# Attention nodes: normalising the context in the transposed layout instead of transposing it back and forth on TensorE

## What is computed

```python
for c in range(6):
    q = ew[c, 0] * (nodes[in_q] @ We[eq] + be[eq])
    k = ew[c, 1] * (nodes[in_k] @ We[ek] + be[ek])
    v = ew[c, 2] * (nodes[in_v] @ We[ev] + be[ev])
    scores = einsum('bqhd,bkhd->bhqk', q @ Wq[c], k @ Wk[c]) / 4
    ctx = einsum('bhqk,bkhd->bqhd', softmax(scores), v @ Wv[c])
    nodes[c] = act_w[c] * (ctx @ Wo[c]) + q
x = x + layernorm(nodes[5]) * ln_g + ln_b
```

## Time and profile before

| | |
|---|---|
| median of 3 runs | 1112.06 us (1109.84 to 1112.44) |
| the profiled execution: time, span of its trace | 1111.26 us, 1109.5 us |
| PE, PEld busy | 1052.3 us (95%), 741.3 us (67%) |
| DVE busy | 816.8 us (74%) |
| ACT busy | 727.1 us (66%) |
| POOL busy | 448.0 us (40%) |

### The profile page before, as it was taken

The page is one execution under the profiler, slowest core; times in us unless marked ns, Lnnn a source line. Parts: engine busy times, 40 slices in busy tenths (PEclk is TensorE's granted clock), DMA queues, the critical chain, the costliest instruction groups (busy, mean ns, idle before and its releaser), DMA issues.

```text
span 1109.5 us, 28104 instructions
## 1 busy us (share of the span) xinstructions
PE 1052.3 (95%) x10281; PEld 741.3 (67%) x10281; DVE 816.8 (74%) x1792; ACT 727.1 (66%) x1605; POOL 448.0 (40%) x884
## 2 busy tenths in 40 slices
PE   8888999988999999999999999999999999999984
PEld 4765655545776677777777777677777777777762
DVE  5457777766788877777777788777777777777873
ACT  3346666652676767776776677767776776777674
POOL 3422232333333333343343378833433343333366
PEclk9889999998999999999999999999999999999997
DMA  9000000015765666666766766676667667666630
GB/s 233 3 1 1 1 0 0 1 27 69 103 92 89 94 96 100 91 97 98 98 88 103 98 98 107 111 98 98 89 100 99 95 90 100 102 90 99 98 50 29
DMA packets 83549, 87.02 MB, mean 78 GB/s; under 512 B 11482, under 2 KB 69342, under 8 KB 83422
## 3 DMA queue, kind: packets, MB, share of 16 engines
q1 hardware_dynamic: 81774, 83.17, 50.0%
q0 software_dynamic: 848, 2.11, 0.8%
q10 hardware_dynamic: 800, 0.05, 0.0%
HBM read 6.51 MB, written 2.10 MB: 8 GB/s over the span
## 4 chain that ended last, share of the span: by engine, by line
PE 76%; DVE 9%; POOL 4%; issue 4%; ACT 4%; DMA 1%; SPq 1%; DVEq 0%; ACTq 0%; POOLq 0%
PE bank L1212 67%; PE bank L1575 5%; PE bank L1582 3%; DVE region L1121 1%; DVE region L1053 1%; DMA mst<-mrows 1%; SPq L493 1%; PE bank L1548 1%; DVE region L937 1%; POOL hl L578 1%; DVE region L1048 1%; POOL hl L581 1%; ACT region L771 1%; DVE region L1041 1%; DVE region L1000 0%
## 5 line engine op out<-in xcount | busy, mean ns | idle before, releaser
L1121 DVE TENSOR_REDUCE region<-bank 128x2 f32<-128x512 f32 x768 | 483.6, 683 | 98.0 <-PE bank L1212 87.7
L795 ACT ACTIVATE region<-bank 128x512 f32<-128x512 f32 x768 | 407.0, 599 | 191.9 <-PE bank L1212 185.8
L1212 PE MATMUL bank<-st 48*128 48x256 f32 x3072 | 307.9, 325 | 4.2 <-DVE region L1121 4.2
L578 POOL TENSOR_TENSOR hl<-qk,one_col 128x512 fp32r<-128x512 f32 x96 | 100.0, 1042 | 435.9 <-ACT qk L760 435.7
L1212 PEld LDWEIGHTS bank<-st 48*128 48x128 f32 x3072 | 242.5, 189 | 17.8 <-DVE region L1121 4.6
L1212 PE MATMUL bank<-region 128*32 128x256 f32 (+3 forms) x3554 | 250.0, 378 | 1.8 <-DVE region L1155 0.6
L1212 PEld LDWEIGHTS bank<-region 128*32 128x32 f32 (+2 forms) x3554 | 131.5, 117 | 84.5 <-issue 16.3
L1212 PE MATMUL bank<-mst,ones 64*128 64x512 bf16 x768 | 150.0, 387 | 2.7 <-DMA mst<-mrows 2.7
L581 POOL TENSOR_TENSOR hl<-qk,hl 128x512 fp32r<-128x512 f32 x96 | 122.2, 1273 | 7.5
L1143 DVE RECIPROCAL region<-bank 128x16 f32<-128x16 f32 x96 | 24.7, 257 | 75.0 <-PE bank L1575 75.0
L1212 PEld LDWEIGHTS bank<-mst,ones 64*128 64x128 bf16 x768 | 36.9, 93 | 62.7 <-issue 38.5
(11 more groups left out here) (195 smaller groups left out, 1444.6 us busy)
## 6 DMA issues: line engine op xcount, KB each, us to landing
st<-hl SPq DMA_DIRECT2D x576, 128.0 KB, 4.6
mst<-mrows SPq DMA_DIRECT2D x192, 6.0 KB
out<-xall POOLq DMA_DIRECT2D x15, 128.0 KB, 2.3
xall<-in_L_attn_hidden_states SPq DMA_DIRECT2D x1, 768.0 KB, 8.5
cst<-in_constants SPq DMA_DIRECT2D x1, 514.5 KB, 4.0
xT<-in_L_ffn_Wq SPq DMA_DIRECT2D x1, 384.0 KB
xT<-in_L_ffn_Wk SPq DMA_DIRECT2D x1, 384.0 KB
xT<-in_L_ffn_Wv SPq DMA_DIRECT2D x1, 384.0 KB
```

Source lines behind the costliest of these rows:

```text
L578: pool.tensor_tensor(to[:, 0::2, :], qk[a.n % 2], one_col[:, :].unsqueeze(2).to_broadcast([P, 2, T]), ALU.mult)\
L795: act.activation(to, x_bank(x, k, e)[:, :].rearrange("p (j q) -> p j q", j=2), ACT.Exp).then_inc(B["exp_ok"], 1)
L1121: dve.tensor_reduce(mx[s.n % 2][:, to:to + 2], s_bank(s, k, e)[:, :].rearrange("p (j k) -> p j k", j=2), AX_X, ALU.max, negate=True).then_ ...
L1212: return pe.matmul(o, w, x, start=start, stop=stop, skip_group_check=skip)
```

## The change

Four things are done differently.

- **The context stays transposed.** The columns of v are laid so that in each strip of 32 partitions heads 0 to 3 have their context in partitions 0:16 and their sum in partition 16, and heads 4 to 7 have their sum in partition 0 and their context in partitions 16:32. VectorE spreads the sum over the 32 partitions of its strip with two stream shuffles (one for each half of the bank, from PSUM to SBUF), takes the reciprocal of all 128x512 elements of the result, and multiplies each half by PSUM's context and by a column of zeros and ones (`halves`) that blanks the other half's partitions. GpSimd adds the two halves (`merge`), which gives the transposed context with the heads in the order 0, 4, 1, 5, 2, 6, 3, 7. The rows of `Wo` are loaded in this order by eight more transfers. `copy_raw`, both transposes and `copy_ctxT` go.
- **Copies change engine or place.** The transposed maxima are copied by ScalarE instead of VectorE (`copy_rows`). The node's result is copied in the same slot (`copy_node(d)`) and no longer at the start of the next.
- **TensorE's order.** `project` stands before `project_v`, and waits for the normalised halves (`nrm_ok`), then, ahead of the product with `w_out`, for the merge.
- **The last layernorm.** Its offset `ln_b` is added to the input rows by GpSimd in an earlier slot (`last_offset`), so that the final scaling has one operation less; the store of the result moves behind `split`.

```diff
+    c[:, C_HALVES:C_HALVES + 2] = i[:, None] // DH % 2 == np.arange(2)[None, :]
...
+        recip = cst[:, C_MASK:C_MASK + 2 * T]
...
-            eng.tensor_tensor(fyn, fyn, lng[:, 1:2, :].to_broadcast([P, KT, D]), ALU.add).then_inc(B["fb_ok"].sem, 1)
-            eng.wait_ge(B["fb_ok"].sem, B["fb_ok"].at(f))
...
+            for h in range(H):
+                at = VW * (h % GCOL) + DH * (h // GCOL)
+                sp.dma_start(w_out[at:at + DH, :, :], a["L0_ffn_Wo"][:, DH * h:DH * h + DH, :].rearrange("c d n -> d c n")).then_inc(L["wout_in"], 16)
...
+            def merge(d):
+
+                pool.wait_ge(B["nrm_ok"].sem, B["nrm_ok"].at(d.n))
+                if d.n > 0:
+                    pool.wait_ge(B["node_ps"].sem, B["node_ps"].at(d.n - 1))
+                pool.tensor_tensor(ctxT, recip[:, 0:T], recip[:, T:2 * T], ALU.add).then_inc(B["ctxT_ok"].sem, 1)
+
+            def last_offset(z):
+
+                tiles = xall[:, ds(z.f * KT, KT), :]
+                pool.wait_ge(A["xn2_ok"], ITERS)
+                pool.tensor_tensor(tiles, tiles, lng[:, 1:2, :].to_broadcast([P, KT, D]), ALU.add).then_inc(B["off_ok"], 1)
...
                 if v is not None and v.last and v.n < STEPS - 1:
+                    pool.wait_ge(B["off_ok"], v.f + 1)
                     final_scale(pool, v)
+                if z is not None and z.c == 3:
+                    last_offset(z)
+                if d is not None:
+                    merge(d)
+                if a is not None:
+                    split(a)
...
-            def copy_raw(d):
+            def normalise(d):
 
                 dve.wait_ge(B["pv_ok"], d.n + 1)
                 if d.n > 0:
-                    dve.wait_ge(B["rawT_ps"].sem, B["rawT_ps"].at(d.n - 1))
-                dve.tensor_copy(raw, bank[OUT][:, :]).then_inc(B["raw_ok"].sem, 1)
...
+                    dve.wait_ge(B["ctxT_ok"].sem, B["ctxT_ok"].at(d.n - 1))
+                dve.stream_shuffle(recip[:, 0:T], bank[OUT][:, 0:T], [DH] * 32)
+                dve.stream_shuffle(recip[:, T:2 * T], bank[OUT][:, T:2 * T], [0] * 32).then_inc(B["sums_ok"].sem, 1)
+                dve.wait_ge(B["sums_ok"].sem, B["sums_ok"].at(d.n))
+                dve.reciprocal(recip, recip).then_inc(B["rec_ok"].sem, 1)
                 dve.wait_ge(B["rec_ok"].sem, B["rec_ok"].at(d.n))
-                dve.tensor_tensor(ctxc.rearrange("p t (h d) -> p (t h) d", h=H), t[:, :, 0:DH],
-                                  rec.unsqueeze(2).to_broadcast([P, KT * H, DH]), ALU.mult).then_inc(B["ctxc_ok"].sem, 1)
+                for g in range(2):
+                    of = slice(g * T, g * T + T)
+                    k = dve.scalar_tensor_tensor(recip[:, of], bank[OUT][:, of], halves[:, g:g + 1], recip[:, of], ALU.mult, ALU.mult)
+                k.then_inc(B["nrm_ok"].sem, 1)
...
             def project(d):
                 to, prev = bank[OUT], source(d, GRAPH[d.c]["src"][0])
-                pe.wait_ge(B["ctxT_ok"].sem, B["ctxT_ok"].at(d.n))
+                pe.wait_ge(B["nrm_ok"].sem, B["nrm_ok"].at(d.n))
                 if not d.last:
                     mm(to[:, T:2 * T], w_res[:, d.c, :], prev, stop=False)
+                    pe.wait_ge(B["ctxT_ok"].sem, B["ctxT_ok"].at(d.n))
                     mm(to[:, T:2 * T], w_out[:, d.c, :], ctxT, start=False).then_inc(B["node_ps"].sem, 1)
```

More of the change, by code:

```diff
@@ L145, in build @@
         head_mask = cst[0:QK, C_HEAD:C_HEAD + GH]
+        halves = cst[:, C_HALVES:C_HALVES + 2]
+        recip = cst[:, C_MASK:C_MASK + 2 * T]
         sign_col = cst[:, C_SIGN:C_SIGN + 1]
@@ L258, in build @@
         probT = [carve(KT * H, T) for _ in range(2)]
-        raw = carve(2 * T)
-        rec = carve(KT * H)
-        ctxc = carve(KT, D)
         ctxT = carve(T)
@@ L307, in build @@
         B.update(chain("fin", "frl fra frb frc frd fr_ok fnb_ok fyn_ok"))
-        B.update(chain("fout", "fg_ok fb_ok"))
+        B.update(chain("fout", "fg_ok"))
         A.update(chain("logsig", "zb_ok za_ok e_ok l_ok gl_ok"))
@@ L314, in build @@
         S.update(chain("bias", "bias_ps bias_c bo_ps bo_ok bias_f nb_b nb_ps"))
-        B.update(chain("ctx", "raw_ok rawT_ps rec_ok ctxc_ok ctxT_ps ctxT_ok node_ps"))
+        B.update(chain("ctx", "sums_ok rec_ok nrm_ok ctxT_ok node_ps"))
         a_ps = [sem(f"a_ps{t}") for t in range(TPI)]
@@ L635, in phase @@
                 if v is not None and v.last and v.n < STEPS - 1:
+                    pool.wait_ge(B["off_ok"], v.f + 1)
                     final_scale(pool, v)
+                if z is not None and z.c == 3:
[4 more added lines that the diff above has]
+                    split(a)
+                if v is not None and v.last and v.n < STEPS - 1:
                     pool.wait_ge(B["out_ok"], v.f + 1)
                     pool.dma_start(out_d[v.f], xall[:, v.f * KT:v.f * KT + KT, :]).then_inc(B["out_stored"], 16)
-                if a is not None:
-                    split(a)
             pool.wait_ge(L["ln_in"], 32)
@@ L809, in copy_vals, with copy_rows @@
                 act.activation(v[:, :, :, 0:DH], bank[IN][:, 0:T].rearrange("p (k h d) -> p k h d", k=KT, h=H), ACT.Copy).then_inc(B["vals_ok"], 1)
-            def copy_ctxT(d):
-                act.wait_ge(B["ctxT_ps"].sem, B["ctxT_ps"].at(d.n))
-                act.activation(ctxT, bank[OUT][:, 0:T], ACT.Copy).then_inc(B["ctxT_ok"].sem, 1)
+            def copy_rows(m):
+                act.wait_ge(B["mt_ps"], m.n + 1)
+                old = at_slot(m.n, 2)
+                if old is not None:
+                    act.wait_ge(m_in[old.n % 2], 32 * old.uses(2))
+                act.activation(mrows[m.n % 2][:, :], bank[IN][0:MCOLS, 0:P].bitcast(BF16), ACT.Copy).then_inc(B["mt_ok"], 1)
             def final_rows(z):
@@ L825, in phase @@
             def phase(t, a, s, m, x, d, z, w, v):
-                if z is not None and not z.last:
-                    copy_node(z)
                 if x is not None:
@@ L835, in phase @@
                     copy_xT(TAILS[t - 6], IN)
+                if m is not None:
+                    copy_rows(m)
                 if x is not None:
@@ L843, in phase @@
                     copy_qk(a)
-                if d is not None:
-                    copy_ctxT(d)
                 if x is not None:
                     exps(x, 3)
+                if d is not None and not d.last:
+                    copy_node(d)
                 if m is not None:
@@ L1181, in phase @@
                     maxes(s, 1)
-                if m is not None:
-                    copy_rows(m)
-                if d is not None:
-                    copy_raw(d)
                 if d is not None:
@@ L1619, in phase @@
                     warm(2, OUT)
-                if d is not None:
-                    transpose_raw(d)
                 if a is not None:
                     project_qk(a)
-                if d is not None:
-                    transpose_ctx(d)
                 burst((3,), (3,))
@@ L1628, in phase @@
                     warm(2, OUT)
+                if d is not None:
+                    project(d)
                 if m is not None:
                     project_v(m, a)
-                if d is not None:
-                    project(d)
             slots(pe, first, {0: fold_weights, 1: folded, 2: last_bias})
```

37 lines of the change are left out of this document (8 added, 29 removed).

## The result

The changed kernel takes **1353.9 us** (median; 1351.1 to 1355.6) against 1110.95 us (1107.2 to 1112.4) for the kernel before on the same chip: the ratio is **1.219**, 95% interval 1.215 to 1.223. It is slower by 243 us. The forecast was 1416 us, range 1300 to 1490.

What follows compares the result with a forecast made beforehand. TensorE bounded the kernel before, at 8.45 us per slot; a ring through VectorE's reciprocal would make it 10.51 (1309 us), and TensorE's clock 11.6: 1111.3 + 96 x 3.18 = 1416 us, range 1300 to 1490.

Steps and rivals of the forecast that it cites:

- The reciprocal, the term that decided: VectorE's reciprocal of 512 elements in each slot: 6.25 ns per element plus 0.16 fixed, 3.36 us.
- the rival that read all of the extra time on 16 elements as fixed: VectorE's reciprocal runs at one element a cycle, 0.66 to 0.77 us; kernel 1050 to 1060 us; chance 0.13.
- The ring: Chain every slot must pass, VectorE to GpSimd to TensorE and back to VectorE's first reduction: 10.51 us.
- it adds 0.55 to the ring: On TensorE, v's product now stands behind the wait for the normalised halves, lengthening the chain by 0.55 us.
- does not hold the ring: TensorE's product with v is done at 610.06, before VectorE is free at 610.40, so it sets no bound.
- TensorE alone could do a slot in 7.41: Without transposes and the wait between them, TensorE's slot loses 1.04 of 8.45 us; 96 slots would save 100 us.
- The time at full clock: Whole kernel with slots of 10.51 us and TensorE's clock unchanged: 1309 us; as a rival, chance 0.25.
- What TensorE waits: TensorE idles about 2.6 us per slot before `w_res`, then 0.5 more while GpSimd merges.
- The clock, the term that was mis-sized: TensorE at half clock after its waits: one slot in three, 3.4 us longer each, average slot 11.6 us.
- TensorE has no gap: In a half-clock slot TensorE never idles, so the clock recovers; between none and one slot in two is slow.
- costed at nothing: `copy_rows` on ScalarE, later `split`, eight weight transfers on SyncE and the moved layernorm offset add no time to the forecast.
- The fast rival: VectorE's reciprocal takes 0.66 to 0.77 us, slots 7.8 to 7.9 us, kernel 1050 to 1060 us; chance 0.13.

Runs made afterwards that it cites:

- e3: Changed kernel with the two halves' sums merged by a predicated copy and the reciprocal taken of 256 elements instead of 512: 1208.5 us, ratio 1.086.
- e2: Changed kernel with v's product back in front of the output projection on TensorE: 1308.9 us, ratio 1.178.
- e7: Changed kernel with 32x32 block transposes on VectorE, a reciprocal of 16 elements, no masks, shuffles or GpSimd merge: 1073.8 us, ratio 0.966.
- e4: Changed kernel with eight unread products of ones on TensorE ahead of the output projection, left out in the last slots: 1308.2 us, ratio 1.176.
- e1: Changed kernel with the reciprocal replaced by a multiplication by a constant, so the context is not divided by its sums: 1084.3 us, ratio 0.976.

## Why the prediction was right, and where its numbers were off

**The reciprocal, the term that decided.** Forecast 3.36 us, measured 3.353; fixed part 0.16, measured 0.157 (e3). The choice of the nearest row in size for the fixed part was right, and the rival that read all of the extra time on 16 elements as fixed is out. That the two agree this closely is luck: only some 100 ns of the row are per element, so the other fixed parts that the prediction had at hand, 136 and 209 ns, would have given 4.01 and 1.75 us. The Trainium skill (VectorE: DVE Perf Modes, the walkthrough of the eight-slice pipeline) gives the iterative divide a repeat count of 8; read as eight cycles per element, that makes an estimate of 4.43 us. The measured 6.24 ns per element are six of the cycles of 1.04 ns that the prediction counts in, so that reading of the page does not hold here.

**The ring.** It can be laid beside the forecast, from the slot shown above (642.84 as t = 0):

| part | forecast | measured | from |
|---|---|---|---|
| four reductions | 2.40 | 2.41 | 642.84 to 645.25 |
| shuffles, hand-over | 0.82 | 0.83 | to 646.08 |
| reciprocal, hand-over | 3.46 | 3.39 | to 649.47 |
| multiplications, merge, until `w_out` | 1.85 | 1.73 | 639.13 to 640.86 |
| `w_out`, v | 1.08 | 1.08 | 640.86 to 641.94 |
| first units until the first reduction | 0.90 | 0.90 | 641.94 to 642.84 |
| sum | 10.51 | 10.34 | |

The shuffles are 0.45 us each, not 0.40, and the pair takes 0.79, not 0.72. The hand-overs within VectorE take 0.04 us each where 0.10 were counted, and `w_out` comes 0.12 earlier, since the hand-overs to and from GpSimd are shorter too (0.08 and 0.05 us).

Two steps beside the sum of the ring were off. In the first, "it adds 0.55 to the ring" is true of this ring, but e2 shows that taking v out gives only 0.27, because the ring through the product with v (10.07 us) stands right behind. The prediction found that this product "does not hold the ring", by 0.34 us in its rows, and it gave VectorE some 0.5 us of room per slot (0.44 measured); it turned neither into a second bound.

The second, "TensorE alone could do a slot in 7.41", is 0.38 us too little: e7 measures 7.79. Half of this is the 0.17 us between the two projections and the transposes back that the prediction took for a wait for VectorE: in e7 the two projections still take 1.06 us (607.98 to 609.04), with nothing of VectorE's behind them. The other half is the unit of scores after them, 0.98 us ahead of `w_res` (609.04 to 610.02), where the earlier trace rows has 0.79 ahead of v. This did not touch the forecast, since the ring is longer than either, but it sets what the change can save on TensorE: 0.66 us per slot, some 63 us and not 100.

**The time at full clock.** 1309 us forecast, 1308 in e4. This agreement is in part luck. The ring was 0.17 us too long, 16 us over 96 slots; and the 16 us that the last node's slots and the end take beyond it (table above) were not in the sum.

**What TensorE waits.** `w_res` starts 8.46 us after the slot's first row (641.94 to 650.40), as forecast. The wait is 2.10 us, not 2.6. The last scores end at 6.36 us, where the forecast had 5.91: the last unit is counted to its end (1.01 us), where the forecast took 0.79, the time until a next one could start, and 0.19 us are the projections, as said.

**The clock, the term that was mis-sized.** "I take one slot in three: 10.51 + 1.1" gave 107 us. e4 measures it, but for the last four slots: 46 us of the time, 48 of the slots, 0.5 us per slot. How often the clock falls was about right: in ordinary steps two slots running are slow, 11.6 and 11.7 us, and then five or six take 10.34, so two in seven or eight, where the forecast had one in three. What a slow slot costs was wrong: 1.3 us on average (a pair takes 2.7 us more than twice 10.34), not 3.4. The clock is low for some 3.4 us in each of the two (from 608.2 to 611.6 and again from 618.4 to 621.8, 1.00 between), and this touches the first units and part of the product with v in the first, and `w_out`, v and the first units in the second; the forecast had it low from `w_out` until the product with v ended, by stretches of 10 us in the earlier trace rows. Its reason for the rhythm, that in such a slot "TensorE has no gap", was wrong too: the slot of 11.60 still ends with a wait of 1.83 us. In the eight slots 41 to 48 it is different: there all four products of `project` are of 128 columns, `w_res` is not under the wait for the merge, the wait is 2.7 to 3.0 us, and the clock is low in part of every slot, for 3.4 us, or 6.8 in three of them: 12.1 to 13.5 us against 10.86 in e4, 14 us in eight slots (table above). TensorE in order of time in such a slot, and the busy time in this stretch with its clock:

```profile
750.67 0.46 PE L1222 MATMUL bank<-w_res,region 128*128 128x128 f32 x2 [3.00 <-POOL region L590]
```

```profile
717.50:818.00 100.50, 77.83 (x730) 58.22 (x728) 86.38 (x156) 51.17 (x121) 52.43 (x124) 0.82 0.46 74
```

A gap of 2.1 us cost little clock, one of 2.7 to 3.0 much. The length of the gap alone does not decide: e2 and e3 both leave one of 0.98 to 0.99 us, with a mean clock of 0.96 and 0.99. What does, these runs don't tell.

**The side effects.** `copy_rows` on ScalarE, the later `split` and the weights' eight transfers were costed at nothing, and e1 shows no wait that points to them. The layernorm's offset was not measured apart.

**The fast rival's own number** (1050 to 1060 us) would have been wrong. e1 puts it in effect and gives 1084. With 436 ns in the reciprocal's place the ring would be 10.34 - 2.92 = 7.42 us, below TensorE's own 7.79; slots of 7.79 do occur, but about every other one waits for the maxima's transfer. What in the transfers sets some 8.15 us on average stays open. In one slot of e7, SyncE spends 3.97 us on the issue of six transfers of `st` and 1.55 on two of `mst`, 5.5 of 8.1 us, and a transfer of `st` lands 4.4 us after its issue in the median, 4.6 in the kernel before. In the slot whose wait is shown above, the maxima's rows were ready at 598.72, but SyncE was issuing transfers of `st` until 599.05 and began on those of `mst` at 599.15. Moving a transfer to ScalarE costs more than it brings, and reordering moves the wait. That the shared queue sets the slot is argued, not shown.

## What to carry to other kernels

Before a long elementwise operation replaces a transpose pair, price it per element by its own kind: put a straight line through the shortest row and a neighbour's fixed part, and ask on how many elements it must really run. Here the sums, 16 numbers per row, were spread to 512 first, and the same idea with block transposes and a reciprocal of 16 wins 3.4% where the spread one loses 21.9%. When you remove one wait, list every ring that stands within 0.5 us of it (here the one through the product with v at 10.07 us and VectorE's own work at 9.9, and, once these are gone, the transfers at 8.15 and TensorE's own work at 7.79), since those decide how much of the gain arrives.

## What the runs showed of the hardware

- The reciprocal on VectorE takes 6.24 ns per element and partition (257, 1753 and 3353 ns for 16, 256 and 512 fp32 elements), while a multiplication by a constant of 512 elements takes 436 ns.
- Turning round 32x32 blocks of fp32 on VectorE costs 707 ns for 512 elements per partition from PSUM and 445 ns for 256 from SBUF, the first little more than the copy (669 ns for 512) that the transposes on TensorE needed anyway.
- A stream shuffle of 256 elements from PSUM takes 0.45 us, a second one starts 0.34 us later, and loading its mask takes 0.01 us.
- With a wait of 2.1 us in every slot of 10.34 us, the clock was low for 3.4 us in two slots running out of seven or eight, 1.3 us of time each. Eight products of ones in the gap, 1.90 us of TensorE, kept it at 1.00 wherever they ran and gave back 46 us.
- Starting one small transfer from ScalarE holds it for 0.73 us; in a loop bound at 8.1 us that cost some 35 to 42 us over 96 slots.
